# Smaller blocks for the first 500 chunks of a four-layer graph network, and other weights for dealing them to slots

## What is computed

```python
def _L0(x): # aggregated by head = src
    att = sigmoid(concat([x[src], relation_emb[edge_type]]) @ att_w + att_b)
    return tanh(segment_sum(att * x[dst], src, N) @ W_w.T + W_b)
def _L1(x):
    agg, deg = segment_sum(x[src], dst, N), segment_sum(ones, dst, N)
    return where(deg > 0, agg, x) @ W.T + b
def _L2(x): return segment_sum(x[src] * edge_weight, dst, N)
def _L3(x): return segment_sum(x[src] * (edge_weight_n2 * edge_weight), dst, N)
for L in (_L0, _L1, _L2, _L3):
    x = layernorm(x + L(x))
```

## Time and profile before

| | us |
|---|---|
| median of three runs | 10662.61 (10654.64 to 10670.87) |
| profiled execution | 10667.16, span of its core 10665.4 |
| PE / DVE / POOL / ACT busy | 8239.5 / 7953.8 / 8009.1 / 5860.8 |
| setup, to the first scatter-add of POOL | 106 |
| stage 0, scatter-adds | 106 to 3777 |
| table sums and layer norm | 3777 to 3948 |
| layers l = 0, 1, 2, gathers | from 3948 on, from 6188 on, from 8427 on to 10605 |

### The profile page before, as it was taken

One profiled execution on the slowest core, in us unless ns is written; L12 is line 12 of the kernel. 1 busy time (PEld: TensorE's weight loads), 2 busy tenths in 40 slices (PEclk: granted clock), 3 DMA queues, 4 the chain that ended last, 5 costly groups with the idle time before them and its releaser, 6 DMA issues. The chain is left out here.

```text
span 10665.4 us, 146984 instructions
## 1 busy us (share of the span) xinstructions
PE 8239.5 (77%) x41161; PEld 5534.8 (52%) x41162; DVE 7953.8 (75%) x19923; ACT 5860.8 (55%) x13187; POOL 8009.1 (75%) x7169
## 2 busy tenths in 40 slices
PE   3887888888888745666666689888888799888887
PEld 2444444444444433555555556655556556555556
DVE  7777777777777657665555499988887699888776
ACT  3766555555555435444433278755554587655553
POOL 4788778888888857777777667777777677777775
PEclk7877777777777757777788789999999899999998
DMA  6433333343333341111111111111111111111111
GB/s 157 48 36 37 36 35 39 38 39 38 39 39 39 38 96 29 29 29 28 29 28 28 29 33 29 30 29 29 29 28 27 38 29 29 29 29 29 27 28 33
DMA packets 651809, 397.35 MB, mean 37 GB/s; under 512 B 456994, under 2 KB 563748, under 8 KB 649745
## 3 DMA queue, kind: packets, MB, share of 16 engines
q0 software_dynamic: 445920, 252.47, 19.4%
q1 hardware_dynamic: 201276, 132.08, 4.9%
q10 hardware_dynamic: 3814, 3.37, 0.2%
HBM read 283.23 MB, written 104.16 MB: 36 GB/s over the span
## 5 line engine op out<-in xcount | busy, mean ns | idle before, releaser
L809 POOL DMA_INDIRECT mem<-xt,mem x5175 | 4900.5, 947 | 1651.2 <-issue 1567.3
L730 POOL DMA_INDIRECT table<-mem,idx x1925 | 2998.3, 1558 | 748.6 <-issue 560.9
L1156 PE MATMUL ps<-mem 128*128 128x392 f32 (+5 forms) x6750 | 2609.3, 502 | 157.4 <-DVE mem L1723 70.8
L951 ACT ACTIVATE mem<-iota_f,mem 128x128 f32<-128x128 f32 x4200 | 1319.5, 390 | 2051.8 <-PE ps L1156 1943.3
L1723 DVE TENSOR_TENSOR mem<-mem,ps 128x392 f32 (+3 forms) x3300 | 1915.9, 581 | 461.0 <-PE ps L1156 422.4
L1706 DVE TENSOR_SCALAR mem<-ps,mem 128x392 f32<-128x392 int16 (+5 forms) x4050 | 2173.3, 556 | 0.0
L1196 PE MATMUL ps<-mem 128*65 128x64 f32 (+2 forms) x7590 | 1010.9, 273 | 1349.9 <-DMA mem<-xt,mem 1348.5
L1196 PEld LDWEIGHTS ps<-mem 128*65 128x65 f32 (+2 forms) x7590 | 816.4, 174 | 1884.2 <-DMA mem<-xt,mem 1751.7
L1156 PEld LDWEIGHTS ps<-mem 128*128 128x128 f32 (+1 forms) x6750 | 1112.1, 178 | 745.8 <-issue 352.2
L930 ACT COPY mem<-zero_c 128x564 f32<-128x564 f32 x1260 | 894.9, 732 | 670.0 <-PE ps L1174 341.8
L1014 PE MATMUL ps<-mem 128*128 128x392 bf16 (+2 forms) x2400 | 789.2, 462 | 500.5 <-DVE mem L1467 394.1
(11 more groups left out here) (186 smaller groups left out, 9445.3 us busy)
## 6 DMA issues: line engine op xcount, KB each, us to landing
mem<-xt,mem POOLq DMA_INDIRECT x5175, 2.4
mem<-key_rows SPq DMA_DIRECT2D x385, 160.0 KB, 3.3
table<-mem,idx POOLq DMA_INDIRECT x1925, 3.2
table<-mem POOLq DMA_DIRECT2D x3, 6304.0 KB, 61.4
mem<-table SPq DMA_DIRECT2D x42, 448.0 KB, 5.2
xt<-xs SPq DMA_DIRECT2D x9, 896.0 KB
mem<-in_x_dram SPq DMA_DIRECT2D x415, 16.0 KB, 2.1
w_d<-mem SPq DMA_DIRECT2D x2, 1562.5 KB, 7.7
```

The lines of the kernel that those rows point to most:

```text
L730: pool.indirect_dma_start(out=tables[i % NTAB][:, :], out_offset=bass.IndirectOffsetOnAxis(ap=idx[:, i % (IDXS * GC):i % (IDXS * GC) + 1], ...
L809: pool.indirect_dma_start(out=gbuf[:, o:o + F], out_offset=None, in_=xt[l][:, :], in_offset=bass.IndirectOffsetOnAxis(ap=src_q[q % 2].bitc ...
L951: ins = act.activation(lo_d[:, k * P:(k + 1) * P], iota_f[:, 0:P], ACT.Abs, bias=nslo_q[q % 2][:, c + k:c + k + 1])
L1156: last = pe.matmul(ps_d[b % PSD][:, 0:w], lo_l[:, r * P:(r + 1) * P], blk_l[:, r * DT:r * DT + w], start=(k == 0), stop=(k == parts - 1))
```

## The change

The first three entries of `PARTS` become two and a longer third: chunks 0 to 250 stand in blocks of one chunk with 2 rows, 250 to 320 in (2, 2, 1) with 3 rows, 320 to 700 single with 3 rows. From 700 on nothing changes. The number of blocks goes from 1100 to 1372, and below chunk 1200 from 900 to 1172: where 200 blocks held the first 500 chunks there are now 472. The zone cost of stage 0 goes from 2.4 to 1.3; in the layers the block cost becomes k (0.2 + 0.105 d) + 0.105 d + 0.13 and the zone cost 0.8. The 16-bit offsets of stage 0 move out of `dinfo` into a free partition of a work area, and one row of intermediates into `acc`. In `block_add0` the wait for the previous add hangs on the add itself and no longer stands ahead of it.

```diff
-PARTS = [(0, 200, (5,), 4), (200, 300, (3, 2), 4), (300, 500, (2, 2, 1), 4), (500, 700, (1, 1, 1, 1, 1), 3),
+PARTS = [(0, 250, (1, 1, 1, 1, 1), 2), (250, 320, (2, 2, 1), 3), (320, 700, (1, 1, 1, 1, 1), 3),
...
 BLOCK_END, ZONE_END = trailing_slots(
-    [max(0.17 * k * d, 0.12 * k * d + 0.14 * d + 0.2) for (_, k), d in zip(BLOCKS, ROWS_OF)], 1.5)
+    [k * (0.2 + 0.105 * d) + 0.105 * d + 0.13 for (_, k), d in zip(BLOCKS, ROWS_OF)], 0.8)
...
 BLOCK0_END, ZONE0_END = slots(SEG_OF0, [0.13 * k * d + 0.24 * d for (_, k), d in zip(BLOCKS[:NB0], ROWS_OF)],
-                              2.4, NU, NT0, 8)
+                              1.3, NU, NT0, 8)
...
-        dinfo = sb("dinfo", [1, ND0 + 40 + padded(NCB)], I16)
+        dinfo = sb("dinfo", [1, 40 + padded(NCB)], I16)
...
-        segb0, boff0 = (arena[0:1, rows0 + k * ND0:rows0 + k * ND0 + NB0] for k in range(2))
+        segb0, boff0 = arena[0:1, rows0:rows0 + NB0], acc[0:1, 11200:11200 + NB0]
...
-        offs0_i, bases0_i, cbase_i = (
-            dinfo[:, sum(m[:k]):sum(m[:k + 1])] for m in [(ND0, 40, padded(NCB))] for k in range(3))
+        offs0_i = arena[WD:WD + 1, 4725:4725 + ND0 // 2].bitcast(I16)
+        bases0_i, cbase_i = (dinfo[:, sum(m[:k]):sum(m[:k + 1])] for m in [(40, padded(NCB))] for k in range(2))
...
             v.memset(dinfo[:, :], 0)
+            v.memset(offs0_i, 0)
...
                 at = win_t[:, :, :, ds(offs0.value(b), rows)]
-                if b:
-                    v.wait_ge(d0_add, b)
                 v.wait_ge(blk0_sum, b + 1)
                 new = ps_pair[b % 2].rearrange("p (t c) -> p t c", t=2)[:, :, 0:rows * T]
-                v.tensor_tensor(at, at, new.rearrange("p t (s d) -> p t s d", s=T), ALU.add).then_inc(d0_add, 1)
+                ins = v.tensor_tensor(at, at, new.rearrange("p t (s d) -> p t s d", s=T), ALU.add)
+                if b:
+                    ins._wait_ge(d0_add, b)
+                ins.then_inc(d0_add, 1)
```

More of the change, by code:

```diff
@@ L355, in program @@
         nq_row = w_in[0:1, 0:Q]
-        assert NSEG <= 32 and NS0 <= 40 and rows0 + 2 * ND0 <= 8455 and rows1 + 32 + NS0 <= 9735
+        assert NSEG <= 32 and NS0 <= 40 and rows0 + ND0 <= 8455 and 11200 + ND0 <= NP and ND0 <= 2 * GE and rows1 + 32 + NS0 <= 9735
         STAGED = AR + 2 * CQ * P + 2 * NTAB * BN
-        offs0_i, bases0_i, cbase_i = (
-            dinfo[:, sum(m[:k]):sum(m[:k + 1])] for m in [(ND0, 40, padded(NCB))] for k in range(3))
+        offs0_i = arena[WD:WD + 1, 4725:4725 + ND0 // 2].bitcast(I16)
+        bases0_i, cbase_i = (dinfo[:, sum(m[:k]):sum(m[:k + 1])] for m in [(40, padded(NCB))] for k in range(2))
         offs_i, cols_i, bases_i = (
```

## The result

The changed kernel takes 10684.93 us (median of 13 runs, 10680.02 to 10698.6), the kernel before beside it 10656.02 (13 runs): ratio **1.0026**, interval 1.0017 to 1.0034, 29 us slower. Slower was forecast, but at 10733. The profiled execution of the changed kernel has a span of 10696.9, against 10665.4 before, 31.5 more.

The account below looks back on a forecast made before the run. POOL's DMA pace bounds the kernel; other engines cost only where POOL waits. Stage 0 +110, layers -43, setup +3 give +70 on 10667.2, 10737, or 10733 at the median; range 10645 to 10800.

Parts of the forecast that it names:

- the size of stage 0, +110: Stage 0 scatters: new small blocks lengthen POOL's waits by 110 us, between +93 and +128.
- the rule: Stage 0: slot work from block and zone prices, against POOL's 9.24 us a slot; excess 48 before, 175 after.
- the old shortfall: Stage 0 of the kernel before: the rule gave 48 us of excess against 82 measured, 34 short.
- part (5): Wait on the add in block_add0: nothing changes for three rows and more; two rows lie in the pitch bounds.
- no deal can hide it: Stage 0, slots 8 to 379: mean slot costs 9.7 us after the change where POOL needs 9.24.
- Layers, -43: Layers 1 and 2: POOL's 43.1 us of waits for PE's aggregation go, -43 us, bounds -20 and -43.
- The setup's +3: Setup: some ten row operations get 272 more elements at about 1 ns, +3 us.
- A: Stage 0 offset loads become cheap through dinfo's move, eight about 0.7 us; about -44, 10619 us; chance 0.07.
- B: Stage 0 small block cheap, old shortfall doesn't recur; excess 113 at 0.75 a block, -9, 10654 us; chance 0.17.
- C: TensorE's clock: lighter PE gets half clock more often, zones lengthen; +135, 10798 us; chance with D 0.16.
- D: Stage 0 small block costs what the three-row one does; excess 223, 10798 us; chance with C 0.16.

Follow-up runs that it names:

- measured prices: Changed kernel with stage 0's deal pricing blocks at (0.08 d + 0.04) k + 0.13 d + 0.49: 10656.56 us, ratio 0.9997.
- short loads: Stage 0 offsets in ginfo, 32-bit: changed kernel 0.9979, with old layer weights 10627.37 us; old blocks with all else new 10584.9 us, 0.9929.
- the 32-bit loads: Changed kernel with stage 0 offsets as 32-bit values loaded four at a time from the same work area: 10638.01 us, ratio 0.9977.
- all but the blocks: Kernel before with the zone cost, attached wait and layers' weights, old PARTS: 0.9944 of 11768.03 on the slow-gather chip; 10605.11 us, 0.9949 on another.

## Why the prediction was right or wrong

**Right.** The way of reading: only POOL's waits count, DVE's pitch per block sets them, and most of the excess comes before slot 100. Forecast and measured, by stretch (slots 8 to 40, 40 to 100, 100 to 150, the rest): 75, 39, 35, 26 against 57, 42, 26, 21. The number of adds (1172), the mean small add (0.658 us for about 0.70), the loads (147 of 1.83 us), L1196's wait (0.6). Smaller than said: the last scatter comes at 3834.5, not 3890; POOL's waits for L884 without the first are 162, not 190; the idle time of the adds under "issue" grew from 68 to 86. That the kernel counts as slower at all is close: 10684.93 lies 1 us above the 10684 where the prediction let "slower" begin.

**Wrong: the size of stage 0, +110 against +58.7 to the last scatter.** It has two steps.

In the forecast the rule's excess for the changed kernel was 175, to which half of the old shortfall of 34 came, 192, against the measured 82. It is 146 against 88. The base was 6 off. With the pitches of the table above the rule gives 61, 29, 29 and 9, or 128, for the changed kernel, 18 below the measured 146, where I had added 17. So the step that failed is the **prices** of the blocks: they took 47 us too much. The blocks' sum is 1417 us, not 1470. Of these 53 some 14 are the small block's own pitch, 0.795 for 0.86 (four fifths of them 0.71, one fifth 1.05 by its place). Some 19 are part (5), "for three rows and more nothing changes": it was costed at nothing, and the attached wait takes 0.13 to 0.23 off every pitch with a load; the run with the standing wait puts its worth at 20.6 us of stage 0. Seven are a slip: 1.37 for a block with four rows holds a bare pitch of 1.27, where the 1.25 worked out beside it gives 1.35; with that the rule's excess is 168, and the forecast some 7 us nearer. The rest is spread: 1.045 us for 1.06 with three rows, 1.24 for 1.25 with four, 1.21 for the 1.36 that the 1.45 of the few blocks of two chunks holds.

That the old shortfall sat in the deal, and not in the rule, is what the new zone cost alone speaks for: the old blocks then lose 65 us, and for that deal the rule gives 66, though not slot by slot (0, 0, 36, 30 against 1, 11, 36, 16 by stretch). So that my 17 came near the 18 now missing is luck: they are half of a miss that belonged to the old deal. Where the 18 come from is open; they are gone when the same blocks are dealt by measured prices (113 by the rule, 111 measured).

**Wrong in its reason: "no deal can hide it".** The sum over all slots was right with these loads (the best deal tried still lost 111 against 88), but two fifths of the blocks' price was the deal, and most of it the load that each eighth block brings (the two overlap): with short loads the blocks cost 35 us, not 92.

**Layers, -43 against about -35.** The waits are gone as forecast, and by the weights, which I hadn't set apart from the blocks. Runs on the same kind of chip give 2 x 17.5 us less gather time (2160 for 2177.6); the rest of the 42.5 is given back as the ordinary gap that a gather without a wait has (issue 1567 us before, 1575 with the 32-bit loads). In the profiled execution 29 show, and 25 with the 3.9 more of l = 0, because gathers take 949 ns on that chip for 947. This miss has the other sign and hides a part of the first: 51 us too much in stage 0, 18 too much gain in the layers of that execution. The setup's +3 was -1.1.

**The rivals.** A fell as put: the move left the load at 1.83. But its question was the good one, since the place does matter, and its price held: with short loads the new blocks lose 69 us for its 78. B came halfway (146 for its 113): the small adds follow each other in 0.795, just under its sign of 0.8, but its prices of 0.75 and 0.80 count the load in, and with the load the block takes 0.94. C's condition came true and its price didn't: between 206 and 504 us TensorE is granted 0.57 of 2.4 GHz where it was 0.87, and PE is busy for 206 us where it was 237. The first line is the changed kernel, the second the one with the measured prices:

```profile
206.00:504.00 298.00, 206.25 (x967) 117.83 (x968) 234.64 (x795) 195.53 (x355) 211.03 (x137) 0.57 0.32 31
206.00:504.00 298.00, 212.81 (x1020) 129.23 (x1019) 236.09 (x839) 193.10 (x354) 248.93 (x161) 0.57 0.39 37
```

(PE, PEld, DVE, ACT, POOL busy, then PEclk.) Zones within a slot follow each other at 1.24 us in the mean between 206 and 560 us where they did at 1.25. And with measured prices the clock is the same 0.57 while the loss until slot 40 is 1 us for 57, so the clock isn't what cost those slots. D is excluded by the pitch.

## What to carry to other kernels

Price a small block with its share of everything that comes once per so many blocks, here a register load that is longer than the work beside it; with the new blocks, shortening that load was worth 78 us, and going back to the old blocks after that only 35. A planner's costs are part of the change: whoever changes the shape of the work measures its pitch and enters that. And where a rule misses the measured time of the kernel before, find out whether the miss belongs to what the change replaces, before carrying it over.

## What the runs showed of the hardware

A register load of DVE costs 0.229 us a value from dinfo and from partition 64 of the work area (16 bit, eight at a time), 0.241 from that partition (32 bit, four at a time) and 0.086 from ginfo (32 bit, four at a time), the last in stage 0 and in the layers alike. Whether 16-bit values in ginfo would be as fast wasn't tried.

An f32 add over runs of two neighbouring elements takes 0.575 us for 392 elements when each run lies in one 16-byte line and 0.968 when it is cut; with three elements 0.77 and 0.955, with four 0.967 whole, 0.983 cut in halves, and 1.04 cut one to three. A cut run of two or three thus takes as long as a whole run of four. The Trainium skill's Advanced Engine Details and Errata, "Memory Cachelines", says that SBUF has 16-byte cachelines and that at least two hits on a line are needed for full speed; the trace agrees for runs of two to four, and the run of four loses little when both lines get two. It doesn't for runs of five: their 980 elements take 1.17 us wherever they lie, though at two of the four offsets one line gets a single element.

On one chip the kernel before takes 11768 us instead of 10660, and the versions that also ran elsewhere have stage 0 unchanged there. POOL waits some 450 times for what the profile calls remote, which doesn't appear on the other chips, and longer for L1196 (all but the blocks, 243.8 us for 2.1):

```profile
POOL mem L809 <- issue: 1412.6, 4616, 1.5
POOL mem L809 <- remote: 1001.5, 452, 6.7
POOL mem L809 <- PE ps L1196: 243.8, 104, 8.5
```

Its cause is open; ratios between kernels agree on both (0.9924 and 0.9929, 0.9944 and 0.9949).
